# Six pairs with row products, statistics shared by ScalarE and VectorE, away rows dealt out anew

## The chip, the core and the metric

The kernel runs on one core of a Trainium2 chip. The time is the device time of one execution in microseconds, the median of the runs shown. TensorE (PE; PEld is its weight load) does matmuls into PSUM, VectorE (DVE), ScalarE (ACT) and GpSimd (POOL) work on elements, and SyncE (SP) issues the transfers. Each engine takes its instructions in the order in which they are written, and waits at a semaphore where one isn't yet high enough.

## What is computed

```python
def _L0_conv_ref(x, W):                 # W: 64 x 64 x 3 x 3
    bw = cw + stop_gradient(sign(W) - cw)      # so the weights are sign(W)
    return conv(x, bw, stride 1, padding 1)
def _gn(v, G=32, eps=1e-05):            # groups of two channels
    return (g - mean(g)) / sqrt(var(g) + eps)
x = x + _L0_conv_ref(_gn(x), L0_conv_W)        # x: 32 x 64 x 56 x 56, float32
```

Each image is normalised over pairs of channels and 56 x 56 points, convolved with the signs of the weights, and added to itself.

## The kernel before

Two images make a pair: 2 x 64 channels fill the 128 partitions, and there are NP = 16 pairs (LAST = 15). The slot of a pair in `xbuf` (eight slots) is loaded in four pieces, changed in place and stored from there.

Statistics: VectorE takes `bn_stats` over seven blocks of 448 elements of a pair (`pair_stats`), exchanges them between the two channels of a group and aggregates (`aggregate`). ScalarE takes the square root (`deviation`, line 413), and VectorE makes scale and shift (`scale`, into `coef`). For pair k + 2 the statistics are made in round k of VectorE's loop, `deviation(k + 1)` is in round k of ScalarE's, and `scale(k + 1)` stands first in round k of VectorE's.

Upper and lower halves: ScalarE writes the normalised rows once as float16 (`hi`, into `halves`) and once as float32 (`normalise`, into `xnorm`), in two chunks of rows for most pairs. GpSimd subtracts the two to the lower half (`lo`). TensorE multiplies both with the weights. So each matmul of the convolution is issued for the upper and for the lower half.

TensorE works in quadrants of 64 x 64. "Home" rows are those whose result lies in the half of the partitions where their image lies, "away" rows come out in the other half, so both kinds run beside each other (`step`, line 738). A pair has home units and away units, and a unit has two PSUM banks. A unit waits in `wait_bank` until the unit two before it of its kind has been taken out of its banks. VectorE adds home units into `xbuf` (`add_home`, lines 544 and 556). An away unit is either added by VectorE in two halves of the partitions (`add_away`, line 570), or copied by ScalarE to `moved` (`move_away`, line 437, two buffers) and added by GpSimd (line 345). `by_scalar(k, i)` decides: in a pair without products VectorE has unit 0 and ScalarE unit 1, in a pair with products the other way round. A bank copied by ScalarE is free when the copy is done.

Pairs in WINOGRAD = (3, 6, 9, 12, 14) compute rows 25 to 42 by products: GpSimd makes sums and differences of rows (`make_lines`, into `lines`: DIFF, STEP and SUM, 2016 elements for a partition), ScalarE scales them to float16 (`line_halves`) and to float32 (`lines_norm`) in parts of 1512 and 504 elements (`line_upper`, lines 447 to 456), GpSimd subtracts (`lo_lines`, line 371). TensorE runs four products of 504 columns for two rows at a time, where six row-products would be due without them. VectorE adds them into odd and even rows: `add_inner` four times, `add_outer` twice (line 587). Products come second and third among the home units. The other home rows are 43 to 55, and the away rows are 0 to 24.

The last pair is direct, with its last two units cut to blocks of 7, 4 and 3 rows that VectorE adds and SyncE stores one after the other (`add_last`).

SyncE loads pair k + 3 in its round k, after away blocks of TensorE have ended, then stores the second part of pair k - 1 and the first part of pair k. All these wait in one queue.

The order of the loops in which the change moves things, before:

```python
# ScalarE, round k                         # VectorE, round k
move_away(k - 2, 1)   # not WINOGRAD       scale(k + 1)
hi, normalise         # all chunks         add_home(k-1, 1)  or  add_outer, add_away(k-1, 1)
line_upper(k)         # WINOGRAD           pair_stats(k + 2)
deviation(k + 1)                           add_home(k, 0); add_away(k, 0)  # not WINOGRAD
move_away(k - 1, 0)   # k-1 in WINOGRAD    aggregate(k + 2); add_inner(k)  # WINOGRAD
```

## Time and profile before

| | |
|---|---|
| median of 3 runs | 201.85 us (201.57 to 202.32) |
| span of the profiled execution | 200.7 us |
| TensorE matmul, weight load | 191.2 us (95%), 168.4 us (84%) |
| VectorE | 165.3 us (82%) |
| ScalarE | 149.7 us (75%) |
| GpSimd | 166.7 us (83%) |
| granted TensorE clock | 1.000 in the mean |
| traffic with HBM | 257 GB/s over the span |

Busy shares are means over the whole span. A timeline gives start and length of an instruction (several of one kind in a row are merged and have a count xN), and in brackets the idle time before it with what ended it. The waits say for whom an engine was idle. The table by stretches gives, after the stretch's limits and length, the busy time (and number of instructions) of PE, PEld, DVE, ACT and POOL, then the granted clock as a share of full speed, the share of DMA engines busy, and GB/s.

### The profile page before, as it was taken

What the parts mean: (1) busy time and instruction counts of PE and PEld (TensorE: products, weight loads), DVE (VectorE), ACT (ScalarE), POOL (GpSimd) and SP (SyncE); (2) the same over time, 40 slices, a digit from 0 to 9 for tenths busy, and PEclk for the clock granted to TensorE, in tenths of its full rate; (3) what the DMA queues carried; (4) which work ended last, traced back from release to release, by engine and by line L of the source; (5) the groups of instructions that cost most, each with busy time, mean ns of one, the idle gap of its engine ahead of it and who ended that gap; (6) DMA issues with size and microseconds to landing.
All of it is one profiled execution on the core that took longest, in us unless ns stands there. A gap on an engine that the chain in (4) does not pass through costs nothing.

```text
span 200.7 us, 10042 instructions
## 1 busy us (share of the span) xinstructions
PE 191.2 (95%) x4482; PEld 168.4 (84%) x4482; DVE 165.3 (82%) x363; ACT 149.7 (75%) x142; POOL 166.7 (83%) x85
## 2 busy tenths in 40 slices
PE   1999999999999999999999999999999999999990
PEld 0478888879858988988999988899998999889990
DVE  2799999996999997799988779998779999627392
ACT  3185999799989289899909989972998999595000
POOL 1029786999999999999999997999999899999500
PEclk9999999999999999999999999999999999999999
DMA  6978977871787988868697887868887883906274
GB/s 216 362 217 292 331 246 252 289 209 44 306 243 291 297 316 282 282 248 278 242 301 296 275 327 276 325 228 321 326 241 296 266 319 152 381 13 238 116 283 175
DMA packets 18698, 52.17 MB, mean 260 GB/s; under 512 B 2080, under 2 KB 5024, under 8 KB 18656
## 3 DMA queue, kind: packets, MB, share of 16 engines
q1 hardware_dynamic: 18656, 51.54, 72.9%
q8 instruction: 35, 0.57, 1.1%
q14 instruction: 7, 0.06, 0.1%
HBM read 25.84 MB, written 25.69 MB: 257 GB/s over the span
## 4 chain that ended last, share of the span: by engine, by line
PE 65%; ACT 14%; DVE 13%; DMA 3%; issue 1%; SPq 0%; DVEq 0%; ACTq 0%
PE psum L738 65%; ACT halves L424 5%; DVE stats L500 5%; ACT xnorm L418 4%; DMA xbuf<-in_x_dram 3%; ACT moved L437 3%; DVE xbuf L570 2%; DVE xbuf L556 1%; DVE xbuf L580 1%; DVE own L508 1%; ACT line_halves L447 1%; ACT std L413 1%; DVE xbuf L544 1%; ACT lines_norm L451 1%; DVE halves L538 1%
## 5 line engine op out<-in xcount | busy, mean ns | idle before, releaser
L738 PE MATMUL psum<-halves,w_taps 64*64 64x385 f16 (+8 forms) x4140 | 183.4, 325 | 0.5 <-DVE halves L532 0.4
L738 PEld LDWEIGHTS psum<-halves,w_taps 64*64 64x64 f16 x4140 | 156.7, 107 | 19.3 <-ACT moved L437 0.9
L330 POOL TENSOR_TENSOR halves<-xnorm,halves 128x784 f16<-128x784 f32 (+5 forms) x35 | 91.6, 2637 | 20.0 <-ACT xnorm L418 19.7
L500 DVE BATCH_NORM_STATS2 stats<-xbuf 128x6 f32<-128x448 f32 x112 | 60.8, 613 | 4.3 <-DMA xbuf<-in_x_dram 4.1
L424 ACT ACTIVATE halves<-xbuf,coef 128x784 f16<-128x784 f32 (+5 forms) x35 | 50.7, 1449 | 3.0 <-DVE coef L525 2.8
L418 ACT ACTIVATE xnorm<-xbuf,coef 128x784 f32<-128x784 f32 (+5 forms) x35 | 50.5, 1443 | 0.0
L437 ACT ACTIVATE moved<-psum 64x784 f32<-64x784 f32 (+1 forms) x30 | 25.5, 850 | 7.9 <-PE psum L738 7.3
L345 POOL TENSOR_TENSOR xbuf<-xbuf,moved 128x784 f32<-128x784 f32 (+1 forms) x15 | 29.3, 1956 | 0.4 <-ACT moved L437 0.4
L570 DVE SCALAR_TENSOR_TENSOR xbuf<-psum,xbuf 64x784 f32<-64x784 f32 (+1 forms) x32 | 28.2, 881 | 1.0
L556 DVE SCALAR_TENSOR_TENSOR xbuf<-psum,xbuf 128x784 f32<-128x784 f32 x21 | 20.3, 967 | 7.6 <-PE psum L738 7.4
L371 POOL TENSOR_TENSOR line_halves<-lines_norm,line_halves 128x1512 f16<-128x1512 f32 (+1 forms) x10 | 20.9, 2120 | 0.5 <-ACT lines_norm L451 0.5
L738 PE MATMUL psum<-line_halves,w_products 64*64 64x504 f16 (+1 forms) x180 | 20.8, 373 | 0.0
L587 DVE SCALAR_TENSOR_TENSOR xbuf<-psum,xbuf 128x504 f32<-128x504 f32 x30 | 18.6, 673 | 1.5 <-PE psum L738 1.5
L413 ACT ACTIVATE std<-own,eps 128x1 f32<-128x1 f32 x16 | 4.6, 287 | 14.8 <-DVE own L508 14.8
L358 POOL TENSOR_TENSOR lines<-xbuf 128x1008 f32<-128x1008 f32 x5 | 11.7, 2337 | 0.0
L651 PE MATMUL psum<-filler 64*64 64x448 f16 x84 | 7.3, 508 | 4.2 <-DMA xbuf<-in_x_dram 4.2
L544 DVE SCALAR_TENSOR_TENSOR xbuf<-psum,xbuf 128x392 f32<-128x392 f32 (+3 forms) x13 | 6.2, 508 | 5.9 <-PE psum L738 5.8
L738 PEld LDWEIGHTS psum<-line_halves,w_products 64*64 64x64 f16 x180 | 10.0, 107 | 0.7
L651 PEld LDWEIGHTS psum<-filler 64*64 64x64 f16 x84 | 3.5, 154 | 7.1 <-DMA xbuf<-in_x_dram 4.2
L508 DVE BATCH_NORM_AGGREGATE own<-stats 128x2 f32<-128x84 f32 x16 | 8.5, 534 | 0.6
L517 DVE RECIPROCAL inv<-std 128x1 f32<-128x1 f32 x16 | 2.6, 161 | 7.1 <-ACT std L413 7.1
L451 ACT ACTIVATE lines_norm<-lines,coef 128x1512 f32<-128x1512 f32 x5 | 7.7, 1542 | 0.0
(36 smaller groups left out, 72.0 us busy)
## 6 DMA issues: line engine op xcount, KB each, us to landing
xbuf<-in_x_dram SPq DMA_DIRECT2D x48, 448.0 KB, 4.6
out_dram<-xbuf SPq DMA_DIRECT2D x43, 392.0 KB, 4.0
xbuf<-in_x_dram SPq DMA_DIRECT2D x16, 224.0 KB, 4.1
out_dram<-xbuf SPq DMA_DIRECT2D x5, 504.0 KB, 3.9
out_dram<-xbuf SPq DMA_DIRECT2D x5, 448.0 KB, 3.8
out_dram<-xbuf SPq DMA_DIRECT2D x5, 364.0 KB, 4.1
out_dram<-xbuf SPq DMA_DIRECT2D x5, 252.0 KB, 4.1
out_dram<-xbuf SPq DMA_DIRECT2D x1, 224.0 KB, 3.8
```

The source lines that it names most:

```text
L330: nc.gpsimd.tensor_tensor(at(halves[:, k % HRING, 1, :], a, b), at(xnorm[:, k % NRING, :], a, b), at(halves[:, k % HRING, 0, :], a, b), AL ...
L345: nc.gpsimd.tensor_tensor(away, away, part, ALU.add).then_inc(add_done, 1)
L358: nc.gpsimd.tensor_tensor(lines[:, DIFF], at(xbuf[:, s, :], WROW - 1, WROW + WROWS - 1), at(xbuf[:, s, :], WROW + 1, WROW + WROWS + 1), AL ...
L371: nc.gpsimd.tensor_tensor(line_halves[:, 1, some], lines_norm[:, some], line_halves[:, 0, some], ALU.subtract).then_inc(line_lo_ready, 1)
L418: nc.scalar.activation(at(xnorm[:, k % NRING, :], a, b), at(xbuf[:, s, :], a, b), ACT.Identity, bias=coef[:, s, 1:2], scale=coef[:, s, 0:1 ...
L424: nc.scalar.activation(at(halves[:, k % HRING, 0, :], a, b), at(xbuf[:, s, :], a, b), ACT.Identity, bias=coef[:, s, 1:2], scale=coef[:, s, ...
L437: nc.scalar.mul(moved[here, m % 2, 0:len(unit) * size].rearrange("p (n m) -> p n m", m=size), psum[there, bank:bank + len(unit), 0:size], ...
L500: nc.vector.bn_stats(stats[:, n, :], xbuf[:, s, n * STAT:(n + 1) * STAT]).then_inc(blocks_ready, 1)
L556: nc.vector.scalar_tensor_tensor(both_rows, psum[:, bank:bank + 2, 0:BN], 1.0 / SCALE, both_rows, ALU.mult, ALU.add).then_inc(home_done, 1)
L570: nc.vector.scalar_tensor_tensor(part[here], made[there], 1.0 / SCALE, part[here], ALU.mult, ALU.add).then_inc(away_done, 1)
L587: return nc.vector.scalar_tensor_tensor(part, made, factor / SCALE, part, ALU.mult, ALU.add)
L738: mm = pe.matmul(outs[:, :, left:right], weights, ins[:, :, left + dx:right + dx], start=first_step, stop=last_step)
```

## The change

- Pair 15 joins WINOGRAD. Its home units are seven rows, the products, then three and three rows. Its away units are 16, 6 and 3 rows. The stores of the last pair are ordered anew.
- Of pairs 8 and 11 four of the seven blocks of statistics, and of pairs 14 and 15 six, are made by ScalarE: two passes over their elements, the first with the sum of x/n, the second with the sum of squared differences (`stats_by_scalar`). They stand in ScalarE's round k - 1 behind the first chunk (or both in a pair with products). The result is put beside VectorE's in `mixed`, whose constant counts GpSimd sets at the start.
- Away units are listed for VectorE in BY_VECTOR, and all others go through ScalarE and GpSimd: unit 0 of pairs 2, 4, 5, 7, 8, 10, 11 and 13 goes from VectorE to them, and (13,1) and (14,0) go to VectorE.
- In ScalarE's round the copy of (k-1,0) stands before the last chunk in a direct pair, and before the product lines in a pair with products. The deviation of pair k + 1 is last.
- In VectorE's round `aggregate(k + 2)` stands behind `add_inner(k)` and the last blocks of statistics.
- Product lines: two buffers. The SUM line is made by VectorE with the mean already taken off. ScalarE makes one pass for the upper half and one, in place, for the float32 values, over all 2016 elements. GpSimd subtracts in one piece. For pairs 14 and 15 VectorE computes the lower half from the raw lines, and the pass in place is left out.

The diff, cut to what is spoken of:

```diff
-WINOGRAD = (3, 6, 9, 12, 14)
+WINOGRAD = (3, 6, 9, 12, 14, 15)
+LINES_BY_VECTOR = (14, 15)
+BY_VECTOR = {(0, 0), (1, 0), (3, 1), (6, 1), (9, 1), (12, 1), (13, 1), (14, 0), (14, 1)}
+SCALAR_BLOCKS = {8: 4, 11: 4, 14: 6, 15: 6}
...
         if k == LAST:
-            return [[(0, 7), (14, 7)], [(28, 7), (42, 4)], [(50, 3)]]
+            return [[(WROW + WROWS, 7)], [2, 1], [0, 3], [(WROW + WROWS + 7, 3)], [(WROW + WROWS + 10, 3)]]
...
         if k == LAST:
-            return [[(7, 7), (21, 7)], [(35, 7), (46, 4)], [(53, 3)]]
+            return [[(0, 8), (8, 8)], [(16, 6)], [(22, 3)]]
...
-        return k != LAST and i == (0 if k in WINOGRAD else 1)
+        return k != LAST and (k, i) not in BY_VECTOR
...
+                if k == LAST:
+                    wait_away(k, 0)
+                    store(k, 0, 0, 16)
+                    sp.wait_ge(home_done, home_before(k) + 3)
+                    store(k, 1, WROW, WROW + WROWS + 7)
+                    sp.wait_ge(home_done, home_before(k) + 4)
+                    wait_away(k, 1)
+                    store(k, 2, 16, 22)
+                    store(k, 3, WROW + WROWS + 7, WROW + WROWS + 10)
+                    sp.wait_ge(home_done, home_before(k) + 5)
+                    store(k, 4, WROW + WROWS + 10, H)
+                    wait_away(k, 2)
+                    sp.dma_start(at(both(out, k), 22, WROW),
+                                 at(xbuf[:, k % XRING, :], 22, WROW)).then_inc(last_stored, 16)
+                    return
...
+            for n in mixed:
+                nc.gpsimd.memset(mixed[n][:, 0, 0, 0:1], float(n * STAT)).then_inc(counts_set, 1)
...
             for k in range(NP):
-                if k >= 2 and k - 2 not in WINOGRAD and k != WINOGRAD[0]:
+                if k >= 2 and by_scalar(k - 2, 1):
                     add_away(k - 2, 1)
-                for c in range(len(chunks(k))):
+                last = len(chunks(k)) - 1
+                for c in range(last):
                     if (k, c) != (0, 0):
                         lo(k, c)
...
+                if k in WINOGRAD:
+                    lo(k, last)
+                if k >= 1 and by_scalar(k - 1, 0):
+                    add_away(k - 1, 0)
+                if k not in WINOGRAD:
+                    lo(k, last)
+                elif k not in LINES_BY_VECTOR:
+                    lo_lines(k)
                 if k == 0:
                     weights_of_products()
                 if k + 1 in WINOGRAD:
                     make_lines(k + 1)
-                if k in WINOGRAD:
-                    lo_lines(k)
-                if k - 1 in WINOGRAD:
-                    add_away(k - 1, 0)
...
+                act.wait_ge(lines_made, 2 * n + 2)
+                act.wait_ge(sum_made, n + 1)
+                if n >= 2:
+
+                    act.wait_ge(home_conv, last_product(WINOGRAD[n - 2]))
+                nc.scalar.activation(line_halves[:, n % 2, 0, :], lines[:, n % 2, :], ACT.Identity,
+                                     scale=coef[:, k % XRING, 0:1]).then_inc(line_hi_ready, 1)
+                if k not in LINES_BY_VECTOR:
+                    act.wait_ge(line_hi_ready, n + 1)
+                    nc.scalar.activation(lines[:, n % 2, :], lines[:, n % 2, :], ACT.Identity,
+                                         scale=coef[:, k % XRING, 0:1]).then_inc(line_norm_ready, 1)
+
+            def stats_by_scalar(k):
+
+                s, n, done = k % XRING, scalar_blocks(k), scalar_stats_before(k)
+                into = mixed[n][:, 0, 0, :]
+                for p in range(n // 2):
+                    act.wait_ge(loaded[s][p], landed(k))
...
+                part = xbuf[:, s, 0:n * STAT]
+                unused = halves[:, k % HRING, 1, 0:n * STAT]
+                nc.scalar.activation(unused, part, ACT.Identity, scale=1.0 / (n * STAT),
+                                     accum_out=into[:, 1:2]).then_inc(scalar_mean, 1)
+                act.wait_ge(scalar_mean, done + 1)
+                nc.scalar.activation(unused, part, ACT.Square, bias=into[:, 1:2], scale=-1.0,
+                                     accum_out=into[:, 2:3]).then_inc(scalar_stats, 1)
...
-                for c in range(len(chunks(k))):
+                last = len(chunks(k)) - 1
+                for c in range(last):
                     if (k, c) != (0, 0):
                         hi(k, c)
                         normalise(k, c)
                 if k in WINOGRAD:
+                    hi(k, last)
+                    normalise(k, last)
+                if k + 1 in SCALAR_BLOCKS:
+                    stats_by_scalar(k + 1)
+                if k >= 1 and by_scalar(k - 1, 0):
+                    move_away(k - 1, 0)
+                if k not in WINOGRAD:
+                    hi(k, last)
+                    normalise(k, last)
+                if k in WINOGRAD:
                     line_upper(k)
                 if k + 1 < NP:
                     deviation(k + 1)
-                if k - 1 in WINOGRAD:
-                    move_away(k - 1, 0)
...
+            def sum_line(k):
...
+                nc.vector.scalar_tensor_tensor(lines[:, n % 2, SUM].rearrange("p (r w) -> p r w", w=W),
+                                               pairs_of_rows[:, :, 0:W], coef[:, s, 2:3], pairs_of_rows[:, :, W:],
+                                               ALU.add, ALU.add).then_inc(sum_made, 1)
+
+            def lo_lines(k):
+                n = winograd_before(k)
+                dve.wait_ge(line_hi_ready, n + 1)
...
+                nc.vector.scalar_tensor_tensor(line_halves[:, n % 2, 1, :], lines[:, n % 2, :], coef[:, k % XRING, 0:1],
+                                               line_halves[:, n % 2, 0, :], ALU.mult, ALU.subtract).then_inc(line_lo_ready, 1)
...
                 if 1 <= k < NP - 1:
                     scale(k + 1)
...
+                if k >= 1:
+                    if k - 1 in WINOGRAD:
+                        add_outer(k - 1)
+                    else:
+                        add_home(k - 1, 1)
+                    if not by_scalar(k - 1, 1):
+                        add_away(k - 1, 1)
+                if k in LINES_BY_VECTOR:
+                    lo_lines(k)
+                if k + 1 in WINOGRAD:
+                    sum_line(k + 1)
+                begun = 2 if k in WINOGRAD else 4
+                if 1 <= k < NP - 2:
+                    pair_stats(k + 2, range(begun))
                 add_home(k, 0)
-                if k not in WINOGRAD:
+                if k != LAST and not by_scalar(k, 0):
                     add_away(k, 0)
...
+                if k in WINOGRAD:
+                    if k < NP - 2:
+                        pair_stats(k + 2, range(begun, begun + 2))
+                        begun += 2
+                    add_inner(k)
                 if k == 0:
                     pair_stats(2, range(NSTAT))
+                elif k < NP - 2:
+                    pair_stats(k + 2, range(begun, NSTAT))
                 if k < NP - 2:
                     aggregate(k + 2)
-                if k in WINOGRAD:
-                    add_inner(k)
...
+            add_away(LAST, 0)
+            add_outer(LAST)
+            add_home(LAST, 3)
+            add_away(LAST, 1)
+            add_home(LAST, 4)
+            add_away(LAST, 2)
```

## Rows read from the trace of the kernel before

**Rows 1.** First part of the page: busy us, share of the span, instructions.
```profile
PE 191.2 (95%) x4482; PEld 168.4 (84%) x4482; DVE 165.3 (82%) x363; ACT 149.7 (75%) x142; POOL 166.7 (83%) x85
```

**Rows 2.** Waits: who waited for whom, us in total, times, longest us.
```profile
ACT std L413 <- DVE own L508: 14.8, 7, 3.7
...
PEld psum L738 <- ACT moved L437: 0.9, 4, 0.4
```

**Rows 3.** Stretches: pair 11, 12, 15, rest; busy PE, PEld, DVE, ACT, POOL; clock, DMA.
```profile
139.07:150.89 11.82, 11.82 (x296) 11.27 (x291) 8.83 (x18) 11.07 (x11) 11.29 (x6) 1.00 0.81 272
150.89:161.41 10.52, 10.52 (x235) 9.44 (x228) 9.87 (x25) 10.09 (x9) 9.27 (x5) 1.00 0.83 288
183.76:195.90 12.14, 12.13 (x366) 11.60 (x356) 8.39 (x13) 0.00 (x0) 4.55 (x2) 1.00 0.45 171
195.90:200.70 4.80, 0.00 (x0) 0.00 (x0) 1.01 (x4) 0.00 (x0) 0.00 (x0) 1.00 0.46 175
```

**Rows 4.** Timeline of VectorE: start us, us, line, operation, [idle before].
```profile
13.04 1.03 DVE L538 TENSOR_TENSOR halves<-xnorm,halves 128x840 f16<-128x840 f32 x1
...
76.93 0.97 DVE L556 SCALAR_TENSOR_TENSOR xbuf<-psum,xbuf 128x784 f32<-128x784 f32 x1 [1.29 <-PE psum L738]
...
77.94 1.98 DVE L570 SCALAR_TENSOR_TENSOR xbuf<-psum,xbuf 64x784 f32<-64x784 f32 x2
...
92.43 0.15 DVE L517 RECIPROCAL inv<-std 128x1 f32<-128x1 f32 x1
...
93.38 1.26 DVE L587 SCALAR_TENSOR_TENSOR xbuf<-psum,xbuf 128x504 f32<-128x504 f32 x2
...
94.67 1.39 DVE L570 SCALAR_TENSOR_TENSOR xbuf<-psum,xbuf 64x504 f32<-64x504 f32 x2
...
196.32 0.69 DVE L580 SCALAR_TENSOR_TENSOR xbuf<-psum,xbuf 64x168 f32<-64x168 f32 x2
```

**Rows 5.** Timeline of ScalarE, rounds 4 to 7 mostly.
```profile
0.74 1.28 ACT L407 ACT_TABLE_LOAD   x1 [0.74 <-PEq L778]
...
57.15 1.85 ACT L437 ACTIVATE moved<-psum 64x896 f32<-64x896 f32 x2
...
71.10 1.66 ACT L437 ACTIVATE moved<-psum 64x784 f32<-64x784 f32 x2 [1.17 <-PE psum L738]
...
75.79 1.03 ACT L424 ACTIVATE halves<-xbuf,coef 128x784 f16<-128x784 f32 x1
...
77.66 1.54 ACT L447 ACTIVATE line_halves<-lines,coef 128x1512 f16<-128x1512 f32 x1
...
80.55 0.79 ACT L454 ACTIVATE line_halves<-lines,coef 128x504 f16<-128x504 f32 x1
...
84.61 1.74 ACT L424 ACTIVATE halves<-xbuf,coef 128x1624 f16<-128x1624 f32 x1
...
90.97 0.28 ACT L413 ACTIVATE std<-own,eps 128x1 f32<-128x1 f32 x1
...
91.27 1.85 ACT L437 ACTIVATE moved<-psum 64x896 f32<-64x896 f32 x2
```

**Rows 6.** Timeline of GpSimd, rounds 3 and 4.
```profile
40.48 2.34 POOL L358 TENSOR_TENSOR lines<-xbuf 128x1008 f32<-128x1008 f32 x1
...
42.79 1.26 POOL L360 TENSOR_TENSOR lines<-xbuf 128x504 f32<-128x504 f32 x1
...
44.01 4.60 POOL L330 TENSOR_TENSOR halves<-xnorm,halves 128x1456 f16<-128x1456 f32 x2
...
48.56 1.87 POOL L345 TENSOR_TENSOR xbuf<-xbuf,moved 128x784 f32<-128x784 f32 x1
...
50.37 4.19 POOL L371 TENSOR_TENSOR line_halves<-lines_norm,line_halves 128x1512 f16<-128x1512 f32 x2
...
56.33 6.34 POOL L330 TENSOR_TENSOR halves<-xnorm,halves 128x1624 f16<-128x1624 f32 x2
```

**Rows 7.** Timeline of TensorE, pair 3: first matmul on a lower product line.
```profile
53.90 0.38 PE L738 MATMUL psum<-line_halves,w_products 64*64 64x504 f16 x2
```

More of the change, by code:

```diff
@@ L175, in conv_preact_kernel @@
         stats = sb("stats", [128, 2 * NSTAT, 6], F32)
+        mixed = {n: sb(f"mixed{n}", [128, 2, 1 + 2 * (NSTAT - n), 3], F32) for n in sorted(set(SCALAR_BLOCKS.values()))}
         own = sb("own", [128, 2], F32)
@@ L307, in _ @@
                 store_unit(k, 0)
-            for n, (first, rows) in enumerate(((28, 14), (42, 8), (50, 6))):
-                sp.wait_ge(home_done, home_before(LAST) + 2 + n)
-                sp.wait_ge(away_done, 2 * (aways_before(away_before(LAST) + 1) + 1 + n))
-                store(LAST, 2 + n, first, first + rows)
             for k in range(NP - XRING, NP):
@@ L467, in _ @@
             for k in range(NP):
[L469 removed]
+                if k >= 2 and by_scalar(k - 2, 1):
                     move_away(k - 2, 1)
[L471 removed]
+                act.wait_ge(coef_ready, 2 * (k + 1))
                 if k >= HRING:
@@ L550, in add_home @@
                 if k in WINOGRAD:
-                    (first, rows), (second, fewer) = home_units(k)[i]
-                    add_rows(k, bank, first, rows)
-                    add_rows(k, bank + 1, second, fewer).then_inc(home_done, 1)
+                    *begun, (j, (first, rows)) = enumerate(home_units(k)[i])
+                    for before, (first_before, rows_before) in begun:
+                        add_rows(k, bank + before, first_before, rows_before)
+                    add_rows(k, bank + j, first, rows).then_inc(home_done, 1)
                     return
```

167 lines of the change are left out of this document (88 added, 79 removed).

## The prediction

> **What bounds the kernel now.** Busy shares first [rows 1]: TensorE is busy 95% of the span, the other engines 75 to 83%. Then who waited: from the start of pair 4 on, TensorE's weight loads lost 0.9 us in four waits for ScalarE's copies of away rows [rows 2]. Then the table by stretches [rows 3], cut at the first matmul of a pair: a direct pair holds TensorE 11.82 us, a pair with products 10.52, busy for all of it and at the full clock. So TensorE sets the time up to its last matmul at 195.9 us, every eviction just fits, and 4.8 us of last additions and stores follow [rows 3, 4]. Whatever makes one pair start late moves the end by as much. I call T5 the start of pair 5 on TensorE, and round 7 of an engine the pass k = 7 of its loop. T5 is 70.75: ScalarE sees the end of pair 4 at 71.10 [rows 5], and a pair's first matmul starts some 0.35 us before its predecessor's end is seen.
>
> **The likely gain.** Pair 15 with products: 11.82 - 10.52 = 1.3 us less TensorE work [rows 3]. The other edits move work between engines that are not the bound, so what counts is the order in their queues.
>
> **What is added to ScalarE.** A pass over 784 elements takes 1.03 us and one over 1624 takes 1.74 [rows 5], so 0.85 ns for each element more. Statistics of four blocks are two passes over 1792 elements, each 1.78 from start to start, with the second waiting for the first: 3.7 us. Six blocks: two passes over 2688, 5.3 us. Neither this form nor its sum output is in the trace. Lower bound: the slope of the product lines, 1.54 us for 1512 and 0.79 for 504 [rows 5], 0.74 ns per element, gives 3.3 and 4.7. Upper bound: a further 0.2 us a pass for the sum, taken from the smallest pass (0.28) [rows 5], gives 4.1 and 5.7. It can't be less than nothing, since the passes are work that wasn't there. I take the first values, from the same tile as source. ScalarE also gets six more away units, 1.68 us each [rows 5]. Its product lines become one pass over 2016 elements, 1.83 us, twice in pairs 3, 6, 9, 12 (3.7), once in 14 and 15.
>
> **What is moved.** In the trace the deviation of pair 8 (line 413) comes at 90.97, before the copy of pair 6's away rows (91.27). In the new loop the deviation is the last instruction of a round, behind the statistics, that copy and the second chunk. VectorE's round begins with scale(k+1), which waits for that deviation. Queued behind it: add_outer (1.27 us) and add_away(k-1,1) (1.42) of a product pair, which free the banks for TensorE's second unit of pair k [rows 4].
>
> **Start, pairs 3 and 4.** GpSimd drops the sum line (start 42.79), but add_away(1,1) now comes ahead of pair 3's lower halves and add_away(2,0) is new: 42.8 + 1.8 + 4.55 + 1.8 = 51.0, then the lower lines in one piece of 4.05, so 55.05 [rows 6]. TensorE wants them at 53.90 [rows 7]: a stall of 1.2. Against it the pause of 0.5 us before pair 4 goes: the copy of pair 3's rows, now behind one chunk instead of two, ends at 58.0 instead of 59.0 [rows 5]. Net +0.6: T5 is 71.4. The two new memsets on GpSimd are hidden in its idle start.
>
> **T5 to T8, and T8 to T11.** ScalarE, from T5 + 0.35. Round 6: copy 1.68, pair 6's chunks 4.87 (to 77.66), copy 1.68, lines 3.7, deviation 0.3, in all 12.2. Round 7: copy 1.68, first chunk 3.3, statistics of pair 8 3.7, copy of (6,0) 1.87, second chunk 3.1 (both chunks 6.36, from 84.61 to 90.97), deviation 0.3, in all 13.95. VectorE after it: scale 0.95, add_outer 1.27, add_away(6,1) 1.42, with gaps 3.75 [rows 4, 5]. Only then TensorE starts the second half of pair 7, 5.9 us. Sum: 0.35 + 12.2 + 13.95 + 3.75 + 5.9 + 0.05 = 36.2 us from T5 to T8, where the trace has 11.82 + 10.52 + 11.82 = 34.15 [rows 3]. Pairs 9 to 11 repeat it: +2.05 twice. GpSimd has 34.0 us of work in the same stretch (lower halves 17.1, five additions 9.4, lines 3.55 and 4.05 [rows 6]) and is late for the product lines by some 0.7 us, but this stall lies inside the 36.2. VectorE's statistics of pair 8 (three blocks left) and its now later aggregate end before round 7 of ScalarE does: hidden, and by 2 us. The sum line, 0.65 us on VectorE in rounds 2, 5, 8 and 11, goes into the time in which it waits for the home rows (1.29 us at 76.93 [rows 4], and it has 2 us of away additions less); without that cover it would cost its length once a period.
>
> **T11 to T14.** Round 12 again 12.2. Round 13 has six blocks instead of four and no other difference: 15.6. Then scale 1.0, and round 14: chunks 4.87, statistics of pair 15 5.3, and only behind these the copy of (13,0), 1.68, for which TensorE's first away block of pair 14 waits. Sum 0.35 + 12.2 + 15.6 + 1.0 + 11.9 = 41.05 us against 34.15: +6.9.
>
> **T14 to T15.** After that copy ScalarE has the upper lines 1.85 and the deviation 0.3; VectorE then scale 1.0, add_home(13,1) 1.0, add_away(13,1) 2.0, lo_lines(14) 2.25. The last I scale from an operation on the same kinds of tiles over 840 elements, 1.03 us [rows 4]: 1176 elements more at 1.03 ns each, VectorE's slope between 504 and 784 columns. TensorE gets the lower lines 8.4 us into the pair, wanted at 6.0. Behind them on VectorE: sum_line(15) 0.65, add_home(14,0) 0.95, add_away(14,0) 2.2 (1.98 for 784 columns, here 896), add_inner 2.45, four of 0.63 with gaps [rows 4]. Pair 15's first bank is free at 14.6 instead of 10.5: +4.1.
>
> **T15 to the end.** VectorE: add_outer(14) 1.27, add_away(14,1) 1.42, lo_lines(15) 2.25. TensorE wants these lower lines at 3.55, since pair 15 has one block ahead of its products, and gets them at 4.9. VectorE goes on without pause: add_home 0.6, inner 2.8 (waiting for the products), add_away(15,0) 2.2, outer 1.3, home 0.35, away of six rows 1.05, home 0.4, away 0.7, with gaps 14.45 us after T15. In the trace it is 197.0 - 183.75 = 13.25 [rows 3, 4]. So the 1.3 us of matmuls saved in pair 15 don't reach the end: +1.2. The last store is smaller (three rows), but in the trace 3.7 us pass between the last addition and the end of the span, mostly latency [rows 3, 4]; I leave that.
>
> **The sum.** 200.7 + 0.6 + 2.05 + 2.05 + 6.9 + 4.1 + 1.2 = 217.6 us of span. The median is 201.85, 1.15 above the profiled span, so 218.8. SyncE: the stores of direct pairs now wait for GpSimd's added (k,0), about one pair later; the loads behind them run three pairs ahead and the DMA share is 0.8 [rows 3], so I cost them nothing. If that cover failed, VectorE's statistics would wait for loads, some microseconds more. Statistics at their bounds move the total by -2.0 or +1.6, as each counts in full.
>
> **A rule against this reading.** ScalarE is busy 149.7 us [rows 1]. With 18 for statistics and 10 for copies, less 3 for lines and 1.5 for chunks it comes to 173, below TensorE's 191. The Trainium skill (Perfetto Trace Analysis, Identifying the Most-Contended Engine) says that one should take the engine with the highest occupancy as the bottleneck and optimise it first. By it TensorE stays the bound. Here occupancy misleads, I think, since the chains above cross two engines.
>
> **Rivals.** (A) The chains have slack that I don't see, TensorE stays the bound, and the time is 201.85 - 1.3 = 200.5, faster. Its place is ScalarE's round 7 and its like. It decides if rounds 6 and 7 take 24.1 us together instead of 26.15, thus if the statistics of four blocks take 1.65 us, and those of six some 3.5 less each. For it: ScalarE waits 14.8 us in the trace for VectorE's variance [rows 2]. Against it: those waits lie mostly in rounds 5, 8 and 11, not in the ones now filled, and one pass alone takes over 1.65.
> (B) Only the end suffers. ScalarE catches up in rounds 8 and 11, and VectorE's order leaves add_away earlier than I place it: without 0.6 + 4.1 it is 214.1.
> (C) Square and Sqrt need different tables. A load is 1.28 us [rows 5], two for each of the four statistics: 2.6 + 2.6 + 5.1 on the chain, 229. Against it: Sqrt, Sign, Copy and Identity share one load in the trace, the only one there. The Trainium skill (ScalarE: Activation LUTs, What ACT_TABLE_LOAD costs) puts a switch at about 2.66 us with its drain, which would make the time some 240; no row here shows a second switch.
>
> **How the numbers follow.** Forecast 0.72, A 0.13, B 0.10, C 0.05. The forecast's own range is 216 to 221. To hold 8 in 10 the range takes in B and missed waits on loads: 211 to 223. It leaves out A and C. The measurement can tell about 0.5% (1 us). Faster 0.12 (A), same 0.03 (A with half its gain eaten by the start), slower 0.85.
>
> **What would show it.** Right: pairs 7, 10 and 13 take 13 to 14 us on TensorE and wait in their middle for VectorE's half-height additions; pairs 13 and 14 wait at their start for ScalarE's copies; the deviations of pairs 8 and 11 come 3 to 4 us after the start of pairs 7 and 10; the pass over 1792 elements takes 1.8 to 2.0 us. Wrong: TensorE without gaps up to pair 12, then the statistics are cheaper or the deviations earlier than I have them. VectorE done within 13.3 us of pair 15's start would refute the last step.

## The result, and the profile after

The changed kernel takes 222.87 us in the median of four executions (222.4 to 223.72), the kernel before on the same chip 201.71 (201.52 to 202.32). The ratio is 1.103, with a 95% interval of 1.099 to 1.106. The profiled execution has a span of 220.9 us and took 222.73.

The first part of its page, with the granted clock over 40 slices and the chain that ended last by engine:

```profile
PE 196.3 (89%) x4422; PEld 159.1 (72%) x4422; DVE 159.7 (72%) x332; ACT 173.7 (79%) x160; POOL 172.8 (78%) x84
...
PEclk9999999999999999999999999999999997997998
...
PE 31%; ACT 26%; DVE 18%; issue 12%; POOL 8%; DMA 3%; SPq 0%; ACTq 0%; DVEq 0%; POOLq 0%
```

Beside [rows 1]: ScalarE went from 149.7 to 173.7 us, GpSimd from 166.7 to 172.8, and VectorE fell by 5.6. No engine is busy for 90% of the span, and the kernel is 10% slower. Nobody is "the bound" by its busy share; TensorE holds only 31% of the chain that ended last, and the rest passes from engine to engine.

Who waited, of the whole execution (us in total, times, longest):

```profile
DVE inv L606 <- ACT std L462: 25.8, 15, 4.3
...
PEld psum L853 <- POOL line_halves L418: 5.1, 4, 1.4
PEld psum L853 <- ACT moved L486: 5.0, 3, 3.4
...
PEld psum L853 <- DVE line_halves L712: 2.3, 2, 1.4
```

In [rows 2] TensorE's loads lost 0.9 us for ScalarE's copies and nothing worth a row for product lines. The direction of one wait has turned: before, ScalarE waited 14.8 us for VectorE's variance; now VectorE waits 25.8 us for ScalarE's deviation, which stands last in its round.

The table by stretches, for pairs 12, 13, 14, 15 and the rest (columns as in [rows 3]):

```profile
155.71:167.68 11.97, 11.01 (x234) 8.70 (x226) 6.18 (x16) 11.84 (x11) 11.97 (x5) 1.00 0.69 231
167.68:181.57 13.89, 12.34 (x292) 9.80 (x288) 6.09 (x13) 12.82 (x12) 12.17 (x6) 1.00 0.47 183
181.57:202.23 20.66, 14.68 (x236) 9.57 (x228) 15.52 (x23) 12.32 (x11) 14.30 (x7) 0.83 0.30 119
202.23:215.80 13.57, 11.49 (x300) 9.52 (x300) 12.53 (x18) 0.00 (x0) 0.00 (x0) 1.00 0.30 118
215.80:220.90 5.10, 0.01 (x1) 0.00 (x0) 0.99 (x3) 0.00 (x0) 0.00 (x0) 0.82 0.48 163
```

Pair 12, 10.52 us in [rows 3], takes 11.97, and ScalarE and GpSimd are busy for all of it. Pair 14 takes 20.66. TensorE works 14.68 us there, at a mean clock of 0.83. The starts of the pairs, predicted and measured:

| first matmul of | before | predicted | measured |
|---|---|---|---|
| pair 5 | 70.75 | 71.4 | 71.45 |
| pair 8 | 104.90 | 107.6 | 107.71 |
| pair 11 | 139.07 | 143.8 | 143.89 |
| first away block of pair 14 | - | 184.9 | 184.9 |
| pair 15 | 183.76 | 199.5 | 202.23 |
| last addition ends | 197.0 | 214.0 | 216.85 |
| end of span | 200.7 | 217.6 | 220.9 |

All of the loss up to pair 14 is where it was put. The step from pair 14 to pair 15 is 2.7 us longer than predicted.

### The profile page after: what moved, and what is told of

Read it like the earlier page. It is cut to its first block, busy times and chain, and to the rows that moved or that the text cites. A ratio compares the mean times of both kernels' runs of the same rounds, so it can differ in the third digit from the quotient of the medians.

```text
span 220.9 us, 9936 instructions
## 1 busy us (share of the span) xinstructions
PE 196.3 (89%) x4422; PEld 159.1 (72%) x4422; DVE 159.7 (72%) x332; ACT 173.7 (79%) x160; POOL 172.8 (78%) x84
## 4 chain that ended last, share of the span: by engine, by line
PE 31%; ACT 26%; DVE 18%; issue 12%; POOL 8%; DMA 3%; SPq 0%; ACTq 0%; DVEq 0%; POOLq 0%
PE psum L853 31%; ACT xnorm L467 7%; ACT halves L473 7%; ACT moved L486 5%; DVE xbuf L660 4%; POOL halves L382 4%; ACT halves L518 4%; DVE xbuf L667 3%; DMA xbuf<-in_x_dram 3%; DVE stats L581 2%; DVE line_halves L712 2%; POOL line_halves L418 2%; DVE lines L702 2%; ACT std L462 1%; ACT line_halves L496 1%
## 5 line engine op out<-in xcount | busy, mean ns | idle before, releaser
L853 PE MATMUL psum<-halves,w_taps 64*64 64x385 f16 (+6 forms) x4032 | 189.3, 328 | 7.8 <-ACT moved L486 3.8
L581 DVE BATCH_NORM_STATS2 stats<-xbuf 128x6 f32<-128x448 f32 x84 | 46.4, 611 | 4.2 <-DMA xbuf<-in_x_dram 4.0
L397 POOL TENSOR_TENSOR xbuf<-xbuf,moved 128x784 f32<-128x784 f32 (+1 forms) x21 | 40.0, 1906 | 2.3 <-ACT moved L486 2.3
L486 ACT ACTIVATE moved<-psum 64x784 f32<-64x784 f32 (+1 forms) x42 | 35.2, 837 | 3.6 <-PE psum L853 2.6
L853 PE MATMUL psum<-line_halves,w_products 64*64 64x495 f16 (+1 forms) x216 | 27.4, 388 | 4.7 <-POOL line_halves L418 3.3
L606 DVE RECIPROCAL inv<-std 128x1 f32<-128x1 f32 x16 | 2.6, 163 | 25.9 <-ACT std L462 25.8
L660 DVE SCALAR_TENSOR_TENSOR xbuf<-psum,xbuf 64x504 f32<-64x504 f32 (+4 forms) x24 | 18.7, 778 | 0.8
L418 POOL TENSOR_TENSOR line_halves<-lines,line_halves 128x2016 f16<-128x2016 f32 x4 | 16.1, 4028 | 0.0
L496 ACT ACTIVATE line_halves<-lines,coef 128x2016 f16<-128x2016 f32 x6 | 11.9, 1976 | 3.8 <-issue 3.7
L702 DVE SCALAR_TENSOR_TENSOR lines<-xbuf,coef 128x504 f32<-128x504 f32 x6 | 12.0, 2004 | 0.0
L853 PE MATMUL psum<-line_halves,w_taps 64*64 64x495 f16 (+1 forms) x72 | 8.9, 382 | 2.1 <-DVE xbuf L631 2.1
```

Of the source, the lines that this page charges most:

```text
L397: nc.gpsimd.tensor_tensor(away, away, part, ALU.add).then_inc(add_done, 1)
L418: nc.gpsimd.tensor_tensor(line_halves[:, n % 2, 1, :], lines[:, n % 2, :], line_halves[:, n % 2, 0, :], ALU.subtract).then_inc(line_lo_poo ...
L486: nc.scalar.mul(moved[here, m % 2, 0:len(unit) * size].rearrange("p (n m) -> p n m", m=size), psum[there, bank:bank + len(unit), 0:size], ...
L581: nc.vector.bn_stats(into, xbuf[:, s, n * STAT:(n + 1) * STAT]).then_inc(blocks_ready, 1)
L660: nc.vector.scalar_tensor_tensor(part[here], made[there], 1.0 / SCALE, part[here], ALU.mult, ALU.add).then_inc(away_done, 1)
L702: nc.vector.scalar_tensor_tensor(lines[:, n % 2, SUM].rearrange("p (r w) -> p r w", w=W), pairs_of_rows[:, :, 0:W], coef[:, s, 2:3], pairs ...
```

## Experiments

Each kernel is an edit of the changed kernel ("after", 222.87 us) or of one named. Times are medians of four executions, unless said. The length of a pause of TensorE is that of its weight loads. The kernel before took 202.1 us beside the first four, 201.76 beside the second four and 202.3 beside the last three.

**1. Statistics back on VectorE.**

```diff
-SCALAR_BLOCKS = {8: 4, 11: 4, 14: 6, 15: 6}
+SCALAR_BLOCKS = {}
```

> The changed kernel with all statistics back on VectorE (an empty table of pairs for ScalarE); everything else as changed. Theory (two chains add up: ScalarE's rounds with statistics up to pair 14, VectorE's queue from pair 14 on): ScalarE's round 7 is 3.9 us shorter, pair 7 runs without a pause, the period T5 to T8 falls from 36.25 to about 35 us (GpSimd's pause at the product lines of 0.8 to 1.4 us stays), pair 14 starts at 176 instead of 181.6, the last part stays long, and the time is 212 to 214 us. Rival 1 (the statistics are all of the loss): 201 to 203 us. Rival 2 (the loss lies in pairs 14 and 15 and the passes only fill idle time): above 217 us.

Measured: 225.07 us (224.4 to 225.44), slower than after. Up to pair 13 all went as expected: pair 8 starts at 105.51, pair 11 at 140.41, and pair 7 has no pause. Then comes this on VectorE's timeline (start, us, line, operation), under it GpSimd's in the same stretch, and TensorE's next wait:

```profile
168.83 14.19 DVE L702 SCALAR_TENSOR_TENSOR lines<-xbuf,coef 128x504 f32<-128x504 f32 x1
```

```profile
166.10 3.08 POOL L382 TENSOR_TENSOR halves<-xnorm,halves 128x1512 f16<-128x1512 f32 x1
169.13 1.27 POOL L409 TENSOR_TENSOR lines<-xbuf 128x504 f32<-128x504 f32 x1
170.35 2.34 POOL L411 TENSOR_TENSOR lines<-xbuf 128x1008 f32<-128x1008 f32 x1
172.63 4.59 POOL L382 TENSOR_TENSOR halves<-xnorm,halves 128x1456 f16<-128x1456 f32 x2
177.17 1.84 POOL L397 TENSOR_TENSOR xbuf<-xbuf,moved 128x784 f32<-128x784 f32 x1
178.96 1.26 POOL L409 TENSOR_TENSOR lines<-xbuf 128x504 f32<-128x504 f32 x1
180.16 2.31 POOL L411 TENSOR_TENSOR lines<-xbuf 128x1008 f32<-128x1008 f32 x1
```

```profile
186.06 8.09 PE L853 MATMUL psum<-halves,w_taps 64*64 64x392 f16 x132 [10.51 <-DVE xbuf L644]
```

A sum line of 504 columns took 14.19 us on VectorE while GpSimd ended one instruction and ran seven more back to back, at the lengths they have elsewhere. It ended at 183.02, 0.55 us after the last of them. Everything behind it in VectorE's queue waited, among it the addition of pair 13's first home unit, whose banks pair 14 needs: TensorE's loads lost 10.9 us. So an effect that I hadn't priced covers the one I meant to measure. The expectation of 212 to 214 missed by 11. The time lies where rival 2 put it (above 217), but not for the reason that rival 2 names. The reason had to be tried by itself (kernels 4, 5 and 6).

**2. Pair 15's sum line a round earlier** (after, with that one line moved on VectorE).

```diff
-                if k + 1 in WINOGRAD:
+                if k + 1 in WINOGRAD and k + 1 != LAST:
                     sum_line(k + 1)
...
                     aggregate(k + 2)
+                if k + 2 == LAST:
+                    sum_line(LAST)
```

> The changed kernel, with VectorE's sum line of pair 15 moved from round 14 to the end of round 13, behind the aggregate of pair 15, where GpSimd has nothing running. Theory (VectorE's operation with two operands in SBUF waits until GpSimd's running instruction ends, and the other way round): the sum line of pair 15 takes 0.6 us instead of 3.43, the first lower chunk of pair 15 on GpSimd stays long only as far as the lower lines of pair 14 cover it, pair 15 starts 3.3 us earlier, and the time is 219.6 us. Rival (the row pattern of this operation is slow by itself, 1.1 to 3.4 us): the sum line stays over 1.8 us at its new place, and the time falls by under 1 us, or not.

Measured: 219.17 us (218.83 to 220.3), ratio to before 1.086 [1.081, 1.091]. The line took 0.74 us at its new place:

```profile
184.21 0.74 DVE L702 SCALAR_TENSOR_TENSOR lines<-xbuf,coef 128x504 f32<-128x504 f32 x1 [0.58 <-DVE coef L599]
```

Pair 15 started at 198.59 instead of 202.23, of which 0.35 us was there before: pair 14's first away block started at 184.54 instead of 184.89. The step between the two is 14.05 us against 17.33 in after. The prediction's 14.6 without its 0.65 for this line is 13.95. So this one line is the whole of the miss in the step.

**3. Additions ahead of the scale in VectorE's round.**

```diff
-                if 1 <= k < NP - 1:
-                    scale(k + 1)
                 if k >= 1:
...
                         add_away(k - 1, 1)
+                if 1 <= k < NP - 1:
+                    scale(k + 1)
```

> The changed kernel, with VectorE's second home and away additions of pair k-1 ahead of the scale of pair k+1 instead of behind it. Theory (ScalarE has too much work in the rounds of pairs with products and after, so the order behind the deviation only picks which engine is late): the pauses in the middle of pairs 7, 10 and 13 vanish (3.3 us of TensorE waits in all), but ScalarE then runs without a break, GpSimd is late for the product lines instead, and the time falls by 0.3 to 1 us, to about 222.2. Rival (what costs is the two additions queued behind the scale, as the prediction's sum says): the pauses vanish and stay gone, 219.5 us.

Measured: 225.12 us (222.1 to 225.32); three executions took 225.0 to 225.3 us, one, without a trace, 222.1. The pauses in the middle of pairs 7, 10 and 13 went, so they were what the prediction said: additions queued behind the wait for the deviation. But the time didn't fall: my 222.2 missed as well. Pairs 6, 9 and 12 got pauses of 2.2, 2.0 and 1.6 us for GpSimd's late lower halves, since the scale now comes later and ScalarE with it. The waits of this kernel:

```profile
ACT halves L473 <- DVE coef L612: 10.8, 6, 3.5
```

It was 5.9 us in after. The rival (the pauses are a loss of their own) falls; they are one face of a ring of waits ScalarE, VectorE, GpSimd, and an edit that breaks it at one place moves the loss to the next.

**4. Statistics of pairs 8 and 11 only.**

```diff
-SCALAR_BLOCKS = {8: 4, 11: 4, 14: 6, 15: 6}
+SCALAR_BLOCKS = {8: 4, 11: 4}
```

> The changed kernel, with ScalarE's statistics kept for pairs 8 and 11 and those of pairs 14 and 15 back on VectorE. Theory: up to pair 12 nothing changes (T12 at 155.7), the pauses at the start of pairs 13 and 14 (1.1 and 3.3 us) vanish, pair 14 starts at 179.5, VectorE's chain in pair 14 still stalls the product lines, pair 15 starts 6 to 7 us earlier, and the time is 216 to 217 us. Rival (VectorE's queue sets the end of pair 14 whatever ScalarE does): within 2 us of the changed kernel, over 220.5.

Measured: no one time. Three executions took 227.56 to 228.88 us, one 212.7. The profiled one (227.97) shows why:

```profile
172.17 14.19 DVE L702 SCALAR_TENSOR_TENSOR lines<-xbuf,coef 128x504 f32<-128x504 f32 x1
```

The same line, the same length, and TensorE's loads waited 10.9 us again; up to pair 13 all went as expected. The expected 216 to 217 us was met by none of the four. The kernel has a race that it sometimes seems to win, and the stake is about 15 us. No trace of the execution of 212.7 us is there, so that its line wasn't held is inferred from its time.

**5. No statistics on ScalarE, and the sum line behind the statistics in VectorE's round** (kernel 1, edited).

```diff
-                if k + 1 in WINOGRAD:
-                    sum_line(k + 1)
                 begun = 2 if k in WINOGRAD else 4
                 if 1 <= k < NP - 2:
                     pair_stats(k + 2, range(begun))
+                if k + 1 in WINOGRAD:
+                    sum_line(k + 1)
```

> All statistics are back on VectorE, and VectorE's sum line of the next product pair stands behind the statistics of the pair after it in the round, so that it is asked for at another moment against GpSimd's run of line instructions. Theory (a sum line that meets a run of GpSimd instructions waits them out; where it meets them decides): no sum line of 14 us; pair 14 starts at 175.6 to 176, pair 15 at 190 to 193 us, 210 to 214 us in all, and the executions agree within 1%. Rival (the 14 us belong to the line's load on GpSimd and not to the moment at which it is asked for): 225 us as with the statistics alone undone.

Measured: two executions of 214.98 and 216.15 us, two of 222.6. In the profiled one (214.98) pair 14 started at 175.31 and pair 15 at 194.09, one us after the range. Pair 14's sum line took 2.25 us and not 14, but two VectorE instructions in a row were held in round 14:

```profile
180.66 4.42 DVE L712 SCALAR_TENSOR_TENSOR line_halves<-lines,coef,line_halves 128x2016 f16<-128x2016 f32 x1
185.01 3.42 DVE L702 SCALAR_TENSOR_TENSOR lines<-xbuf,coef 128x504 f32<-128x504 f32 x1
```

In this execution another place in the queue shortened the wait of the line, as expected. It doesn't make the executions agree: that half of the expectation missed, and since no trace of a 222.6 us execution is there, where those 8 us went is open.

**6. GpSimd waits for the sum line** (kernel 1, with a wait in GpSimd's `make_lines`).

```diff
                 if n >= 2:
                     wait_lines(pool, WINOGRAD[n - 2])
+                if k != LAST:
+                    pool.wait_ge(sum_made, n + 1)
                 made = lines[:, n % 2, :]
```

> All statistics are back on VectorE, and GpSimd starts on a product pair's lines only when VectorE's sum line of that pair has been made, so that the two never want the memory at once there. Theory (the 14 us are VectorE waiting behind GpSimd's back-to-back instructions): no sum line over 2 us but the last pair's, 212 to 214 us in all, the executions agree within 1%. Rival (the sum line waits for something else, such as its own input): 225 us as without the wait.

Measured: 211.27 us (211.02 to 212.32), ratio 1.047 [1.043, 1.051], the executions 0.6% apart. VectorE's sum line of pair 14, and GpSimd's instruction that now waits for it:

```profile
170.30 0.90 DVE L704 SCALAR_TENSOR_TENSOR lines<-xbuf,coef 128x504 f32<-128x504 f32 x1
```

```profile
171.37 1.27 POOL L411 TENSOR_TENSOR lines<-xbuf 128x504 f32<-128x504 f32 x1 [0.71 <-DVE lines L704]
```

```profile
POOL lines L411 <- DVE lines L704: 3.7, 5, 0.8
```

This last row is from its waits. A wait that costs GpSimd 3.7 us in all takes 13.8 us off kernel 1. So the 14 us were VectorE standing behind GpSimd's run of instructions, not a wait for input. The wait orders the line only against `make_lines`: in rounds 5, 8 and 11, where GpSimd was at its lower halves, the line still took 1.82 to 1.83 us. The kernel also gives the nearest price of the statistics: 222.87 - 211.27 = 11.6 us, of which 1.7 is the shorter last sum line (1.74 us here against 3.43). The handshake is in it too, so it isn't quite clean. The time is 0.7 us below the range.

**7. Four blocks instead of six.**

```diff
-SCALAR_BLOCKS = {8: 4, 11: 4, 14: 6, 15: 6}
+SCALAR_BLOCKS = {8: 4, 11: 4, 14: 4, 15: 4}
```

> ScalarE makes four blocks' statistics of pairs 14 and 15 instead of six. Theory (each pass of ScalarE between pairs counts in full for the start of the next): two passes fewer before pair 14 and two before pair 15, 0.9 us each by the rows of the kernel after, so some 1.5 us earlier at each, 3.2 us in all: about 219.7 us. Rival (something else of the round ends as late): less than 1 us, 222 us. If a sum line is passed over by GpSimd's run of instructions as in the kernel without these statistics, 11 us more in those executions, 228 to 231 us.

Measured: 219.59 us (219.2 to 220.17), ratio 1.088 [1.084, 1.092]: 3.3 us less than after. Four passes were shortened by 896 elements each, 0.75 us a pass by the rows of after shown further down (2.43 - 1.68 and 2.54 - 1.79), 3.0 in all. The profiled executions (219.2 and 222.73) are 3.5 us apart, and 0.56 of it was there before the first shortened pass: TensorE got pair 12's lower lines at 162.63 here and at 163.19 in after. That leaves 3.0, so each us of these four passes counted in full.

**8. The old split of away rows** (kernel 5, with VectorE's units as in the kernel before).

```diff
-BY_VECTOR = {(0, 0), (1, 0), (3, 1), (6, 1), (9, 1), (12, 1), (13, 1), (14, 0), (14, 1)}
+BY_VECTOR = {(k, 0) for k in (0, 1, 2, 4, 5, 7, 8, 10, 11, 13)} | {(3, 1), (6, 1), (9, 1), (12, 1), (14, 1)}
```

> As the kernel with the sum line late and no statistics on ScalarE, and the away rows shared between VectorE and GpSimd as in the kernel before, so that what is left of the change is the products of the last pair and the lines normalised in place. Theory (the moved away units bring VectorE's waits in the middle of pairs 7, 10 and 13 and GpSimd's late lines, 0.8 to 1.2 us each in some four places): pair 14 starts at about 174 us, pair 15 at about 184 us, 203 to 206 us in all. Rival (the moved units cost nothing, the product lines of the last pair alone are at fault): within 1 us of the kernel with the sum line late, so 210 to 214 us.

Measured: 206.49 us (206.14 to 206.86), ratio 1.022 [1.019, 1.025], half a microsecond above the range and far from the rival. The pauses at product lines in pairs 6, 9 and 12 are gone: pairs 4 to 13 run at 11.82 and 10.52 us each, in the new order of the loops. So up to there the order by itself costs nothing; it costs when statistics and more copies stand in it. What is left of the loss is in the last two pairs:

```profile
160.60:172.42 11.82, 11.82 (x293) 10.64 (x289) 11.30 (x25) 8.72 (x7) 11.63 (x6) 1.00 0.72 265
172.42:185.16 12.74, 10.95 (x236) 8.01 (x228) 12.14 (x21) 10.27 (x10) 12.74 (x6) 1.00 0.40 157
```

Pair 13 (first line) is as before. In pair 14 GpSimd is busy for all of 12.74 us, and pair 15 then has pauses of 1.9 us (its lower lines) and 1.3 us (a bank at its end) of its own.

**9. The statistics alone** (kernel 8, with them put back).

```diff
-SCALAR_BLOCKS = {}
+SCALAR_BLOCKS = {8: 4, 11: 4, 14: 6, 15: 6}
```

> The kernel with the old split of away rows and the late sum line (206.5 us), with one thing of the change put back: ScalarE makes four or six blocks' statistics of pairs 8, 11, 14 and 15. Theory (ScalarE's passes stand ahead of the pair's normalisation and count in full in the round): the same excess that the statistics have over the kernel in which GpSimd waits for the sum line (222.87 against 211.27, of which 1.7 us is the longer last sum line), so 8 to 10 us more: 214.5 to 216.5 us. Rival (in the old split ScalarE waits 20.0 us in all for VectorE's means, so the passes fill that time): 205.5 to 207.5 us.

Measured: 214.27 us, 7.8 more than kernel 8 and 0.2 below the range; the rival (they fill ScalarE's waits) falls. Three executions took 213.99 to 214.38 us. The fourth took 409.4, at the full clock; it has no trace, and what happened in it is open. The waits for VectorE's means did shrink, from 20.0 to 14.3 us, but in exchange VectorE waits 13.6 for ScalarE's deviation, and pairs 7, 10 and 13 each pause at their start (1.2, 1.3 and 2.8 us) and in their middle:

```profile
173.69 0.53 PE L853 MATMUL psum<-halves,w_taps 64*64 64x392 f16 x8 [0.79 <-DVE xbuf L660]
```

**10. Pair 14's lower lines on GpSimd again** (kernel 8, edited).

```diff
-LINES_BY_VECTOR = (14, 15)
+LINES_BY_VECTOR = (15,)
```

> The kernel with the old split, the late sum line and no statistics on ScalarE (206.5 us), with pair 14's low halves back on GpSimd from lines that ScalarE normalises, as pairs 3 to 12 have them. Theory (VectorE's 2.59 us for them delay its adds and cause the 1.09 us pause in pair 14 at 178.34 and part of that of 1.42 us at 181.16): both go, 204 to 205.5 us. Rival (GpSimd, with 3 us more in round 14, ends the low halves of pair 15 later): 206.5 to 208 us.

Measured: 210.97 us (210.26 to 211.64), worse than kernel 8 by 4.5; both numbers missed, the mechanism of the rival holds. Both pauses in pair 14 went: it took 10.54 us, and pair 15 started at 183.88, 1.3 us earlier than in kernel 8. Then TensorE stood still:

```profile
191.09 1.33 PE L853 MATMUL psum<-halves,w_taps 64*64 64x392 f16 x12 [4.88 <-POOL halves L382]
```

GpSimd's 4.02 us for the low halves of pair 14 (from 174.66) push pair 15's own low halves, and those are held by VectorE's line instruction on top.

**11. Kernel 10 with pair 15's sum line a round earlier** (the edit of kernel 2).

> As the kernel with pair 14's low halves back on GpSimd, with pair 15's sum line at the end of VectorE's round 13. Theory (the 1.84 us pause in pair 15 at 188.63 is VectorE, 2.3 us late with pair 15's low halves because the sum line stood ahead of its adds): the pause goes, 1.5 to 2 us less than that kernel, 202.5 to 204 us, at best level with the kernel before: the products of the last pair save TensorE 1.3 us and cost two further pauses. Rival (the pause waits for something else): within 0.5 us of that kernel.

Measured: 208.2 us (207.83 to 208.69), ratio 1.029 [1.025, 1.033]: 2.8 us less than kernel 10, over the theory's 1.5 to 2, but 4 us above its range of 202.5 to 204, which rested on the time that I had expected of kernel 10. The early line was no bargain here: it met GpSimd's 4.01 us instruction, took 3.10 us, and held the scale of pair 15.

```profile
175.33 3.10 DVE L702 SCALAR_TENSOR_TENSOR lines<-xbuf,coef 128x504 f32<-128x504 f32 x1 [0.21 <-DVE coef L599]
178.36 0.15 DVE L606 RECIPROCAL inv<-std 128x1 f32<-128x1 f32 x1
...
188.26 4.10 DVE L712 SCALAR_TENSOR_TENSOR line_halves<-lines,coef,line_halves 128x2016 f16<-128x2016 f32 x1
```

The pause that was to go is still there, 2.2 us long, since VectorE's lower lines took 4.10 us beside GpSimd. What went is the 4.9 us behind kernel 10's lower halves (0.4 here).

No version with products in the last pair came under the kernel before.

**The account.** From 201.8 us of the kernel before: products in the last pair and the new way to make lines +4.7 (kernel 8). The away rows given to ScalarE and GpSimd +4.8, from kernel 8 to kernel 6; this step also has the handshake and another place of the sum line, so it is no pure price, and without the handshake the sum was 215.0 us or more (kernel 5). The statistics on ScalarE +11.6 (kernel 6 to after), or +7.8 where the away rows are split as before (kernel 9). The two passes of each of the four statistics are 17.8 us of ScalarE's time, so not all of it reaches the end.

In the middle of the kernel the two don't add up. A period of three pairs takes 34.2 us in kernel 8 (as before), 34.9 in kernel 1 (away rows moved), 36.3 in kernel 9 (statistics alone, from the middle of pair 7 to that of pair 10), and 36.2 in after (both). With the statistics there, the moved rows cost nothing in these pairs.

## Why the prediction was right

**The number.** 222.87 us lies 0.13 us inside the top of the range of 211 to 223, and above the forecast's own range of 216 to 221; one execution of the four (223.72) is outside. That it fell inside is luck in part: one term was too small, as told below, and the room that took it up had been given for late loads. The walk up to pair 14 is not luck. The chances weren't quite consistent: A has 0.13 at one place, 0.12 and 0.03 at another.

**What bounds.** "Whatever makes one pair start late moves the end by as much" held. Kernel 7 shows it by dose: 3.0 us of passes less, 3.0 us of time less.

**The price of statistics.** Neither form was in the trace of before. ScalarE's timeline of after, round 7 and round 13:

```profile
89.29 1.68 ACT L518 ACTIVATE halves<-xbuf 128x1792 f16<-128x1792 f32 x1
90.88 0.19 ACT L518 ACTIVATION_READ_ACCUMULATOR halves<-xbuf 128x1 f32 x1
91.10 1.79 ACT L521 ACTIVATE halves<-xbuf,mixed 128x1792 f16<-128x1792 f32 x1
...
93.00 1.85 ACT L486 ACTIVATE moved<-psum 64x896 f32<-64x896 f32 x2
...
161.67 2.43 ACT L518 ACTIVATE halves<-xbuf 128x2688 f16<-128x2688 f32 x1
...
164.22 2.54 ACT L521 ACTIVATE halves<-xbuf,mixed 128x2688 f16<-128x2688 f32 x1
...
166.88 1.85 ACT L486 ACTIVATE moved<-psum 64x896 f32<-64x896 f32 x2
```

From 89.29 the copy starts at 93.00: 3.7 us, as predicted. Six blocks: 161.67 to 166.88, 5.2 against 5.3. The passes are a little shorter than the slope of same-tile chunks gave, and reading out the sum costs an instruction of 0.19 us each; the two errors cancel, which is luck. The bounds of 3.3 and 4.1 held; the 1.8 to 2.0 us named for one pass of 1792 did not (1.68 and 1.79).

**The order in the queues.** The deviation of pair 8 came at 97.98, 3.4 us after pair 7's start, and the rest as walked, on VectorE and then TensorE:

```profile
98.29 0.16 DVE L606 RECIPROCAL inv<-std 128x1 f32<-128x1 f32 x1 [2.40 <-ACT std L462]
...
99.12 1.26 DVE L667 SCALAR_TENSOR_TENSOR xbuf<-psum,xbuf 128x504 f32<-128x504 f32 x2
100.42 1.39 DVE L660 SCALAR_TENSOR_TENSOR xbuf<-psum,xbuf 64x504 f32<-64x504 f32 x2
```

```profile
101.86 0.86 PE L853 MATMUL psum<-halves,w_taps 64*64 64x392 f16 x16 [0.79 <-DVE xbuf L660]
```

From pair 5 to pair 8 it is 36.26 us against 36.2, from pair 8 to pair 11 36.18 against 36.2, from pair 11 to the first away block of pair 14 41.0 against 41.05. The last of the deviations was placed less well: 2.7 us after pair 10's start in the second period, below the 3 to 4 that I gave. Pairs 7 and 13 took 13.1 and 13.9 us. Pair 10 took 12.5 and not 13 to 14, since pair 9 had been longer by its stall; the sum of the two held.

**Start.** +0.6 predicted, +0.70 measured, with a pause of 1.36 us at pair 3's lower lines (1.2 predicted). The loads from HBM, put at nothing, cost nothing: after 20 us no engine waited for one.

**The sum lines: right in the sum, wrong by themselves.** I gave 0.65 us each. They took 1.81, 1.83, 1.91, 1.91, 1.14 and 3.43. The first four cost no start of a pair, as said: they fell in VectorE's wait. The last did.

**The term that was mis-sized: pair 14 to pair 15.** Predicted 14.6 us from the first away block, measured 17.3. The term is "sum_line(15) 0.65". VectorE's timeline, and GpSimd's in the same stretch:

```profile
190.89 2.32 DVE L712 SCALAR_TENSOR_TENSOR line_halves<-lines,coef,line_halves 128x2016 f16<-128x2016 f32 x1
193.13 3.43 DVE L702 SCALAR_TENSOR_TENSOR lines<-xbuf,coef 128x504 f32<-128x504 f32 x1
196.48 0.97 DVE L631 SCALAR_TENSOR_TENSOR xbuf<-psum,xbuf 128x392 f32<-128x392 f32 x2
```

```profile
191.19 4.84 POOL L382 TENSOR_TENSOR halves<-xnorm,halves 128x1456 f16<-128x1456 f32 x1 [0.90 <-ACT xnorm L467]
```

VectorE's line instruction began first, and GpSimd's took 4.84 us; the same shape took 2.96 in kernel 6 with no line instruction beside it. Then GpSimd had the turn, and the sum line ended at 196.56, 0.54 us after GpSimd's at 196.02. In these rows an instruction on two operands in SBUF costs VectorE its own length only if GpSimd isn't in the middle of one of its own when it comes up. That is what the prediction left out; 3.43 - 0.65 = 2.8 us is the miss. Kernel 2, which moved that line alone, started pair 15 3.64 us earlier: 3.3 by the line, and 0.35 by which pair 14 had started earlier. The lower lines of pair 14 took 2.32 us against an estimated 2.25.

The Trainium skill (SBUF — State Buffer, SBUF: two separate sides) states such a rule: the port pair that the two engines share is an exclusive lock, held for the whole instruction by whoever starts first, also for a VectorE instruction with two SBUF inputs against a GpSimd instruction that reads SBUF. These rows agree. The rule speaks of one instruction; that a waiting line is passed over by seven more, as in kernel 1, it doesn't say. I had read [rows 4] and [rows 6] for lengths and not for overlap.

**Pair 15 to the end.** 14.6 us to the last addition against 14.45, so the 1.3 us of matmuls saved in pair 15 didn't reach the end, as said. The tail after it is 4.05 us instead of 3.7, and the profiled execution took 1.83 us beyond its span where the prediction added 1.15. These two make 1.03 us of the 4.07 by which the median lies above 218.8; with the 2.7 above and 0.17 here less than 0.2 is left.

**The rivals.** A (TensorE stays the bound, 200.5) is refuted by every start of a pair from 5 on; its condition, statistics at 1.65 us, was missed by 2 us. B (only the end suffers, 214.1) fell, since rounds 8 and 11 gave nothing back. C (a table switch for each) did not happen: the trace of after has one table load in it, at 0.73. The rule of the most contended engine (the Trainium skill, Perfetto Trace Analysis, Identifying the Most-Contended Engine) would have kept TensorE as the bound. It still is the busiest at 89%, so the trace doesn't contradict its ranking, but busyness names nothing that would have said +21 us. ScalarE's busy sum came to 173.7 against 173 predicted.

## What to carry to other kernels

Where several engines pass work round in a ring, price an added instruction by its place in its engine's queue and by who waits behind it; a free engine by its share (ScalarE at 75%) is not free at that place. Walk one period of the loop from measured lengths: here that gave three stretches of a period each within 0.1 us. And look at every VectorE instruction with two SBUF operands for what GpSimd does at the same time: give them an order by a semaphore, or the kernel can have a lottery in it (212.7 or 228 us for one and the same program).

## What the runs showed of the hardware

- VectorE's line instructions and GpSimd's didn't overlap in effect: where they met, one of the pair was stretched until the other was done. A held sum line of 504 columns ended about 0.55 us after GpSimd's instruction (after, kernels 1 and 4), a held instruction on 2016 columns 2.1 us after it (4.49 us long in kernel 3). Undisturbed, the first takes 0.74 us (kernel 2) and the second 2.32.
- VectorE's instructions with one operand in PSUM and one in SBUF were not stretched: the home additions of 784 columns took 0.95 to 0.98 us in the whole of kernel 1, GpSimd busy or not.
- A held VectorE instruction isn't always next. In kernels 1 and 4 it was passed over at each of seven borders between GpSimd's instructions, for 14.19 us; in kernel 5 and in after it got in after one or two. Both times it was 14.19 us to the last digit, although the kernels differ. What decides it isn't settled: kernel 6 shows only that an order by a semaphore avoids that wait.
- A sum output costs ScalarE an instruction of 0.19 us of its own, and a pass with squares needs no table besides the one of the square root: no second load.
- The granted clock fell after pauses. Two rows of TensorE's timeline of after, 504 columns each, at the higher level (2.4 GHz; the next one starts 0.21 us later) and at the lower (1.2 GHz; 0.42 us later). Between them the clock fell, some 1 us after the pause that ended at 197.50 (2.1 us of the matmuls, 2.6 of the weight loads):

```profile
198.17 0.38 PE L853 MATMUL psum<-line_halves,w_taps 64*64 64x504 f16 x2
...
199.03 0.63 PE L853 MATMUL psum<-line_halves,w_products 64*64 64x504 f16 x2
```

  By the table, first the stretch behind the 3.0 us without a matmul at the start of pair 14, then the end of pair 14, behind the rows above:

```profile
185.00:190.00 5.00, 5.00 (x82) 4.18 (x86) 2.78 (x7) 4.01 (x4) 5.00 (x3) 0.67 0.41 161
...
200.00:202.20 2.20, 1.77 (x20) 0.45 (x12) 2.20 (x5) 0.00 (x0) 0.00 (x0) 0.55 0.52 209
```

  In kernels 6 and 8, whose pauses in pair 14 are 1.5 us at most, it ran at 1.00. Before pair 15 the low clock cost nothing: VectorE's additions there took 3.63 us for six in after, and 3.63 in kernel 2, where the clock was 1.00 in that stretch, so VectorE and not TensorE freed the bank.
